# The maximum pass of a causal attention kernel: both heads of a query block in one unit, as two 64-row bf16 products

## The reference

```python
keys = jnp.einsum('bse,neh->bsnh', residual, W_key) + Bias_key
queries = jnp.einsum('bse,neh->bsnh', residual, W_query) + Bias_query
values = jnp.einsum('bse,neh->bsnh', residual, W_values) + Bias_values
scores = jnp.einsum('bknh,bqnh->bnqk', keys, queries) / jnp.sqrt(jnp.asarray(H, scores_dtype(residual)))
causal_mask = q_idx < k_idx
scores = jnp.where(causal_mask[None, None, :, :], jnp.asarray(EPS, scores.dtype), scores)
probs = jax.nn.softmax(scores, axis=3)
weighted = jnp.einsum('bnqk,bknh->bqnh', probs, values)
```

## Time and profile before

| | us |
|---|---|
| median of 3 runs | 2535.77 |
| the runs | 2529.65 to 2536.67 |
| the profiled execution, its own time | 2534.19 |
| its span, first to last instruction | 2532.4 |
| one pair of heads in the loop (each of the 15 with a background) | 123.37 |
| the opening maximum pass | 50 |

### The profile page before, as it was taken

How to read it: one execution, slowest core, us unless ns; L and a number is a source line. 1 busy time by engine, 2 the same in 40 slices (tenths; PEclk the granted TensorE clock), 3 DMA queues, 4 the chain that set the end, 5 groups by cost and what they waited for, 6 DMA issues and landing times. The chain is left out here.

```text
span 2532.4 us, 30157 instructions
## 1 busy us (share of the span) xinstructions
PE 2288.2 (90%) x10080; PEld 1173.7 (46%) x10080; DVE 1509.9 (60%) x3862; ACT 816.5 (32%) x1166; POOL 1255.4 (50%) x1141
## 2 busy tenths in 40 slices
PE   3479999999999999999999999999999995699987
PEld 2214444444444444444444444444444442577765
DVE  3584756565656565666656565757574754166664
ACT  1113333333333333433333333333333342001111
POOL 0005565657475747474747474747474764111110
PEclk8659999999999999999999999999999997799998
DMA  4464362635354445444353535453535331612100
GB/s 138 142 139 104 79 152 74 151 92 133 97 128 104 120 115 143 124 105 129 97 143 91 141 98 134 99 135 90 135 91 136 82 89 34 220 42 100 59 17 17
DMA packets 205354, 273.58 MB, mean 108 GB/s; under 512 B 69200, under 2 KB 86800, under 8 KB 205200
## 3 DMA queue, kind: packets, MB, share of 16 engines
q1 hardware_dynamic: 205200, 271.67, 40.9%
HBM read 176.69 MB, written 94.63 MB: 107 GB/s over the span
## 5 line engine op out<-in xcount | busy, mean ns | idle before, releaser
L687 POOL TENSOR_TENSOR acc<-acc,probs 128x512 f32<-128x512 f32 (+1 forms) x960 | 1063.7, 1141 | 428.8 <-ACT probs L907 428.7
L907 ACT ACTIVATE probs<-ps_s 128x1024 f32<-128x1024 f32 (+2 forms) x640 | 552.9, 898 | 409.9 <-PE ps_s L772 227.4
L770 PE MATMUL ps_s<-qq,kk 128*128 128x512 f32 (+3 forms) x1280 | 639.6, 500 | 33.6 <-ACT probs L907 33.6
L956 DVE TENSOR_REDUCE partial<-ps_bg 128x1 f32<-128x512 f32 x768 | 514.0, 687 | 197.8 <-PE ps_bg L718 192.2
L791 PE MATMUL ps_o<-probs,v 128*64 128x512 f32 (+3 forms) x2560 | 539.5, 542 | 17.0 <-DVE num L990 17.0
L718 PE MATMUL ps_bg<-k_bf,q_pad 128*128 128x512 bf16 (+3 forms) x1280 | 434.9, 364 | 51.4 <-DVE partial L953 17.8
L772 PE MATMUL ps_s<-qm,kl 128*128 128x512 f32 (+3 forms) x1280 | 469.2, 367 | 0.0
L705 PE MATMUL ps_bg<-xs,w_in 128*128 128x512 f32 x768 | 367.1, 603 | 21.1 <-DMA xs<-xn_turned 18.7
L770 PEld LDWEIGHTS ps_s<-qq,kk 128*128 128x128 f32 x1280 | 247.8, 194 | 196.3 <-issue 119.9
L680 POOL TENSOR_TENSOR acc<-probs 128x512 f32<-128x512 f32 x96 | 120.4, 1275 | 418.7 <-ACT probs L907 418.7
L953 DVE CUSTOM_DVE_ANT_0 junk<-ps_bg,mask_q 128x512 bf16<-128x512 f32 (+3 forms) x512 | 242.4, 486 | 100.0 <-issue 93.9
(11 more groups left out here) (101 smaller groups left out, 1687.8 us busy)
## 6 DMA issues: line engine op xcount, KB each, us to landing
high_and_low<-split SPq DMA_DIRECT2D x128, 512.0 KB, 5.5
qq<-high_and_low SPq DMA_DIRECT2D x64, 512.0 KB, 4.8
kk<-high_and_low SPq DMA_DIRECT2D x128, 256.0 KB, 5.5
qm<-high_and_low SPq DMA_DIRECT2D x64, 256.0 KB, 6.3
kl<-high_and_low SPq DMA_DIRECT2D x64, 256.0 KB, 6.7
e<-masked_weights SPq DMA_DIRECT2D x128, 128.0 KB, 2.9
scale<-inverse_sums SPq DMA_DIRECT2D x128, 128.0 KB, 2.9
heads_turned<-o_out SPq DMA_DIRECT2D x64, 256.0 KB, 2.1
```

The lines of the kernel that those rows point to most:

```text
L687: g.tensor_tensor(acc[h][:, group % 2, q0:q0 + w], acc[h][:, group % 2, q0:q0 + w], probs[h][:, probs_slot(i, t), at:at + w], ALU.add).the ...
L770: pe.matmul(out, kk[:, h, kb * P:(kb + 1) * P], qq[:, h, q], start=True, stop=False, skip_group_check=True)
L907: nc.scalar.activation(probs[h][:, probs_slot(i, t), 0:width], ps_s[:, h, 0:width], ACT.Exp, scale=SCORE_SCALE).then_inc(p_ready, 1)
L956: e.reduce_max(to, ps_bg[:, n % 2, 0:w], AX.X).then_inc(max_read, 1)
```

## The change

- A unit is now (query block, key chunk) for both heads. It has two products: head 0 with partitions 0 to 63 of `q_bf` and `k_bf` into bank 0, head 1 with partitions 64 to 127 into bank 1. There are 40 units with 80 products, each over 64 rows and not 128.
- DVE reads a full unit with one `reduce_max` over 2x512 elements, and a unit on the diagonal with two `tensor_tensor_reduce` in a row.
- `q_pad` becomes `q_bf`: one cast over 128 partitions and not two over 64, and no zeros are written at the start.
- In the loop both banks of `ps_bg` belong to one unit, so unit n waits until unit n-1 is read. `MAX_AT` gives every second slot from 35 to 113: three units a tile, after slots 6t+1, 6t+3 and 6t+5.
- In the opening pass units go in turn to `ps_bg` and to the two halves of `ps_s`; unit n waits for the read of unit n-3, and DVE waits for its own read before a unit on the diagonal.

```diff
--- before.py
+++ after.py
@@ -278,15 +278,16 @@
-MAX_UNITS = [(h, qb, u, min(CH, 128 * (qb + 1) - CH * u))
-             for c in GROUPS for qb in range(4 * c + 3, 4 * c - 1, -1) for u in range(c + 1) for h in range(2)]
+MAX_UNITS = [(qb, u, min(CH, 128 * (qb + 1) - CH * u))
+             for c in GROUPS for qb in range(4 * c + 3, 4 * c - 1, -1) for u in range(c + 1)]
 NMAX = len(MAX_UNITS)
 NPROJ = 12
 PROJ_CHUNKS = [3, 2, 1, 0]
 PROJ_SLOT = [3 * u for u in range(NPROJ)]
 MAX_SLOT = 35
-MAX_AT = [n + (n % 6 == 4) for n in range(MAX_SLOT, MAX_SLOT + NMAX)]
-LAST_MAX = {c: max(v for v in range(NMAX) if MAX_UNITS[v][1] // 4 == c) for c in GROUPS}
+MAX_AT = [MAX_SLOT + 2 * n for n in range(NMAX)]
+LAST_MAX = {c: max(v for v in range(NMAX) if MAX_UNITS[v][0] // 4 == c) for c in GROUPS}
+HEAD = [slice(64 * h, 64 * h + 64) for h in range(2)]
@@ -348,7 +349,7 @@
         xs = sb("xs", [P, 4, halves, CH])
         split = [sb(f"split{b}", [P, 4, CH], F32R) for b in range(2)]
         vt = sb("vt", [P, S])
-        q_pad = [sb(f"q_pad{h}", [P, S], BF16) for h in range(2)]
+        q_bf = sb("q_bf", [P, S], BF16)
         k_bf = sb("k_bf", [P, S], BF16)
         partial = sb("partial", [P, 2, 16, 5])
         neg_max = sb("neg_max", [P, 4, 8])
@@ -436,6 +437,10 @@
         def fin_index(kind, c):
             return [e[:2] for e in FIN].index((kind, c))
+        def max_banks(j, n):
+            return (ps_bg, ps_s[:, 0, :].rearrange("p (h w) -> p h w", h=2),
+                    ps_s[:, 1, :].rearrange("p (h w) -> p h w", h=2))[n % 3 if j == 0 else 0]
+
         def nth(i, group):
             return 4 * i + 3 - group
@@ -707,16 +712,20 @@
                     mm.then_inc(proj_done, 1)
                 def max_unit(j, n):
-                    h, qb, u, w = MAX_UNITS[n]
+                    qb, u, w = MAX_UNITS[n]
                     if n == 0:
                         pe.wait_ge(bf_ready, START + 4 * (j + 1))
-
-                    if n < 2:
                         pe.wait_ge(proj_read, START + NPROJ * (j + 1))
+                    elif j == 0:
+                        if n >= 3:
+                            pe.wait_ge(max_read, START + n - 2)
                     else:
-                        pe.wait_ge(max_read, START + NMAX * j + n - 1)
-                    pe.matmul(ps_bg[:, n % 2, 0:w], q_pad[h][:, qb * P:(qb + 1) * P], k_bf[:, CH * u:CH * u + w],
-                              start=True, stop=True).then_inc(max_scores, 1)
+                        pe.wait_ge(max_read, START + NMAX * j + n)
+                    to = max_banks(j, n)
+                    for h in range(2):
+                        mm = pe.matmul(to[:, h, 0:w], q_bf[HEAD[h], qb * P:(qb + 1) * P],
+                                       k_bf[HEAD[h], CH * u:CH * u + w], start=True, stop=True)
+                    mm.then_inc(max_scores, 1)
                 def turn_max(j, c, before):
                     pe.wait_ge(max_ready, START + 4 * j + (3 - c) + 1)
@@ -937,23 +946,24 @@
                     if m == 0:
-                        for h in range(2):
-                            own = slice(64 * h, 64 * h + 64)
-                            e.tensor_copy(q_pad[h][own, cols(c)], part[own, 0, :].bitcast(F32))
+                        e.tensor_copy(q_bf[:, cols(c)], part[:, 0, :].bitcast(F32))
                     else:
                         e.tensor_copy(k_bf[:, cols(c)], part[:, 2, :].bitcast(F32)).then_inc(bf_ready, 1)
                 def take_max(j, n):
-                    h, qb, u, w = MAX_UNITS[n]
+                    qb, u, w = MAX_UNITS[n]
+                    of = max_banks(j, n)
                     dve.wait_ge(max_scores, START + NMAX * j + n + 1)
                     if u == qb // 4:
+                        if j == 0 and n:
+                            dve.wait_ge(max_read, START + n)
                         e.memset(wait_here[:, n % 4:n % 4 + 1], 0.0)
-                    to = partial[:, h, qb, u:u + 1]
-                    if u == qb // 4:
-                        e.tensor_tensor_reduce(junk[:, n % 2, 0:w], ps_bg[:, n % 2, 0:w], mask_q[:, CH - w:CH], 1.0,
-                                               3 * NEVER, ALU.add, ALU.max, to).then_inc(max_read, 1)
+                        for h in range(2):
+                            mx = e.tensor_tensor_reduce(junk[:, h, 0:w], of[:, h, 0:w], mask_q[:, CH - w:CH], 1.0,
+                                                        3 * NEVER, ALU.add, ALU.max, partial[:, h, qb, u:u + 1])
+                        mx.then_inc(max_read, 1)
                     else:
-                        e.reduce_max(to, ps_bg[:, n % 2, 0:w], AX.X).then_inc(max_read, 1)
+                        e.reduce_max(partial[:, :, qb, u:u + 1], of[:, :, 0:w], AX.X).then_inc(max_read, 1)
                     c = qb // 4
                     if n == LAST_MAX[c]:
                         dve.wait_ge(max_read, START + NMAX * j + n + 1)
@@ -1014,8 +1024,6 @@
                 e.memset(partial[:, :, :, 0:4], 3 * NEVER)
                 e.memset(partial[:, :, :, 4:5], MASKED_RAW)
                 e.memset(ones_row[:, :], 1.0).then_inc(counted, 1)
-                for h in range(2):
-                    e.memset(q_pad[h][:, :], 0.0)
                 e.memset(qm[64:128, :, :].bitcast(F32), 0.0)
                 e.memset(kl[64:128, :, :].bitcast(F32), 0.0)
                 e.memset(ones64[:, :], 1.0)
```

## The result

The changed kernel takes 2572.77 us as the median of four runs, the kernel before 2534.94 in the same session: a ratio of 1.0162, with a 95% interval of 1.0139 to 1.0184. It is slower, where I had forecast 2527 and a small gain. The profiled execution has a span of 2569.5 us against 2532.4, so 37 us are to be found.

A forecast was written before the change was run, and what follows sets the result against it. PE was taken to bound the loop, DVE the opening. On 2534.2 us, +4 for fifteen pairs and -8 for the opening gave 2530, median 2532; 0.3 a pair less made it 2527, range 2492 to 2580.

The forecast's parts named there:

- the switch in the ring: Rival, loop: array shape changes only once the waited-for unit is issued, 0.09 us in 20 joints; 2561, slower, 15%.
- open joints: Loop, some 8 unit-to-unit steps where PE doesn't wait: array switch put at 0.06 us each, 0.5 us a pair.
- DVE's jobs at slot 68: Loop: masked_part and invert (0.74 and 0.55 us), queued ahead of the next read, leave 0.4 us of wait.
- Opening, -8 forecast: Before the loop: opening maximum pass 6 us less (43.7 us), zeros of q_pad gone, 2 us less.
- Products together, -7.9: Loop, PE: a unit's two 64-row products run at the same time, saving 7.9 us a pair.
- The ring, 1.77 and 13.0 of new waits: Loop, PE and DVE in turns: product, read, next product take 1.77 us; waits 13.0 us a pair, replacing 5.3.
- the long joint: Loop, unit step from slot 6t+3 to 6t+5, with `weighted`: PE has 2.19 us of work, no wait, 0.42 over.
- short joints: Loop, unit steps with two score groups: PE has 1.15 us of work and waits 0.62 us in each.
- the narrow tiles: Diagonal tiles at the end of a pair: count thought too dear there, so 0.3 us a pair taken off.
- The clock, 3%, over 2850: Rival, loop: PE's clock falls, 70 us of each pair a third longer or more; over 2850, slower, 3%.
- The short ring: Rival, loop: second product starts with the first, two-bank read takes 1.14 us, ring 1.63; 2485, faster, 13%.
- The halves do run together: Loop, against a rival that 64-row products don't overlap: first unit 0.46 us, +99 us, 2626, slower, 8%.

The follow-up runs named there:

- e5: The changed kernel, with reduce_max in the loop reading only the first half of each bank (2x256 elements, maxima wrong): 2478.69 us.
- e7: The kernel before, with q_bf without zeros and each of its 80 units a single 64-row product of one head: 2674.08 us, 1.0556.
- e4: The changed kernel, with POOL adding only 64 columns of each block in all but a group's first addition (denominators wrong): 2518.51 us.
- e1: The changed kernel, with masked_part of group 2 at slot 64 and not 68: 2539.11 us, 1.0029 to the kernel before.
- e8: The changed kernel, with the old padded 128-row products (q_pad, its casts and zeros) back: 2611.21 us, 1.0311.
- e9: The changed kernel, with masked_part of group 2 at slot 64 and an extra 512-element DVE scan into a spare tile at slot 68: 2586.10 us, 1.0217.
- e3: The changed kernel, with the first unit at slot 36 and not 35, so units follow slots 6t, 6t+2 and 6t+4: 2571.31 us, 1.0152.

## Why the prediction was wrong

The measured 2572.77 us lies inside my range of 2492 to 2580, but by luck: the range reached so far up for the switch in the ring, which did not happen, and I had forecast a gain where there is a loss. Two steps failed, the price of the open joints and, above all, that of DVE's jobs at slot 68, and the clock came on top of the second.

**Opening, -8 forecast.** Right, and a little small. From DVE's first memset to the loop's first projection it was 99.5 us (94.20 to 193.71) and is 89.0 (96.48 to 185.44). 2.1 of these 10.5 are the memsets, 4.6 the pass (130.61 to 175.83, 45.2 us where I had said 43.7), the rest the projections ahead of it and the turns behind it. In this profiled execution the part ahead began 2.3 us later, so 8.3 are seen.

**Products together, -7.9.** Right as a price of the two products, wrong as what PE gains. The first failed step is "in some 8 joints without a wait I put 0.06": it is 0.28 (e5, e7). I measured the switch by the first product behind it alone, 0.32 against 0.23, and did not look at the second one behind, nor at the step in.

**The ring, 1.77 and 13.0 of new waits.** The ring is 1.72 and the long joint 2.19: the 0.05 that I added for a later start of the second product is not there (3 to 4 ns), so the 20 short joints gave 1.0 back. But inside it PE waited 0.28 us (1.72 less the 1.44 of e5) and not the 0.62 I said; the rest is switches, which the ring hid. The two errors, -1.0 for the ring and by estimate +1.8 (8 x 0.22) for eight open joints, partly cancel, which is luck: with POOL cut (e4) a pair is 123.93, against 123.66 by my sum. The 0.5 us between their sum and this 0.3 is not accounted for, and the 0.3 that I then took back for the narrow tiles is not seen.

**DVE's jobs at slot 68, 0.4.** This is the step that made the kernel slower: the joint that follows is 3.86 us, 1.67 more than the other long ones, where the sum has 0.4. Without it the fifteen pairs would have lost some 8.5 us (123.93 against 123.37) and the opening gained 8, so level with the kernel before, and still no gain. I took 0.74 and 0.55 us from the earlier trace rows, which show `masked_part` at 1131.70 in slot 68, but `invert` at 1165, in another slot. In slot 68 of the kernel before, the sum of `invert` took 0.66 us beside POOL, as this row, which I had not shown, says:

```profile
1132.96 0.66 DVE L998 TENSOR_TENSOR total<-den_sq,masked_den 32x32 f32<-32x32 f32 x1
```

There DVE had another read between the two jobs, and two banks in turn, so the lengthening was hidden. That `masked_part` at 1131.70 kept its 0.74 us fits its moment: it began 0.06 us ahead of a POOL addition, and it was the addition that grew, to 1.82 us, where its neighbours took 1.28 and 1.26:

```profile
1131.76 1.82 POOL L687 TENSOR_TENSOR acc<-acc,probs 128x512 f32<-128x512 f32 x1
```

Now both jobs stand in a row, each begun while POOL adds, and the ring waits for them: +1.20 us a pair for `masked_part` (125.57 less 124.37, e1, which moves it away) and +0.44 for the rest (124.37 less 123.93, e4), 25 us in all.

**The clock, 3%, over 2850.** The mechanism came, at another size. I weighed a fall in the whole 70 us of the maximum pass. It fell for 7 us behind one long wait, in five pairs, at 2.35 us each: 12 us.

**The rivals.** The short ring came true by a third (1.72: the second product does start with the first, but the read was 1.23 and not 1.14), "switch paid in the ring" not at all, and its place, the open joints, was counted too low. The halves do run together. That the worst wait would not be in the ring itself but behind a job queued ahead of it was in the sum as 0.4 us and in no rival.

## What to carry to other kernels

When a change makes two engines take turns, list every job of the faster one that stands in a short turn, and read the duration of that job at that very slot, with what POOL does beside it: an operation with two SBUF inputs can take the rest of a POOL operation more. A pair of half-array products pays only where products of its own shape are its neighbours, or where a wait covers the switch. And a wait of more than a microsecond on PE in a stretch that is otherwise full can cost more than its own length again in clock, in some pairs and not in others.

## What the runs showed of the hardware

- **DVE and POOL.** A DVE operation on two SBUF operands that began during one of POOL's additions ended, with few exceptions, at a fixed distance behind the end of that addition, wherever in it it had begun: the 32x32 sum 0.04 us behind it (it took 0.42 and 1.25 us in the changed kernel, 0.66 in the one before, and 0.17 alone), `masked_part` 0.55 behind it (0.81 and 1.31 in the changed kernel, 1.18 in e1, 0.90 in e8, and 0.74 alone). So it stood still until the addition was over and then did its own work. The scan of e9 took 2.31 us and 1.22 alone. An addition that begins just behind `masked_part` is lengthened in its turn (1.82 us). Reads of PSUM (L966, 1.15 to 1.23) were not touched. With POOL's additions cut to 64 columns, the longest of 64 such sums is 181 ns. The Trainium skill (SBUF — State Buffer, section Terms) tells of a port pair that DVE and GpSimd hold for a whole instruction while the loser blocks fully; the ends at 1147.22 and 1147.18 agree with it.
- **Array shape.** Going from 128-row to 64-row products and back costs some 0.28 us over three steps (0.08 in, 0.08 and 0.10 behind; e5 and e7). Two 64-row products of 512 columns in the two halves start 3 to 4 ns apart and take the time of one (0.39 us).
- **Clock.** With PE idle for 1.6 us in the middle of a pair the granted clock fell to 1.2 GHz in 5 of 15 pairs, with 2.5 us in 13 of 15, with 0.4 us in none, and with 1.1 to 1.3 us late in the pair (e3) in 3 of 15; the wait of 1.16 us between two pairs never brought it down. It came back after 6.8 us, or after 3.4 in five pairs of e9 and one of e3.
